# x^T of the first norm by block load and VectorE's block transpose, the norm folded into weights and exponential, and new PSUM places

## What is computed

```python
q, k, v = layernorm(x) @ Wq, ctx @ Wk, ctx @ Wv          # 8 heads of 64
x = x + (softmax(q k^T / 8) v) @ Wo + bo
h = layernorm(x)
rw = gating(h)                                           # softmax over active experts, at least 2
q, k, v = [sum_e rw_e * (h @ W_e) for W in (q_proj, k_proj, v_proj)]
a = softmax(causal(q k^T / 8)) v
x = x + sum_e (rw_e * a) @ o_proj_e
```

## Time and profile before

| | |
|---|---|
| runs, median of 3 | 2540.22 us |
| the profiled execution | 2538.06 us |
| its span, first to last instruction | 2536.3 us |
| mean granted TensorE clock | 0.987 |
| TensorE matmul busy | 2467.8 us, 97% |
| VectorE busy | 2124.7 us, 84% |
| ScalarE busy | 1558.2 us, 61% |
| GpSimd busy | 1102.7 us, 43% |
| TensorE's share of the chain that ended last | 81% |
| DMA queue of SP (q1), packets and share of the 16 engines | 230443, 45.6% |

### The profile page before, as it was taken

How to read it: one execution, slowest core, us unless ns; L and a number is a source line. 1 busy time by engine, 2 the same in 40 slices (tenths; PEclk the granted TensorE clock), 3 DMA queues, 4 the chain that set the end, 5 groups by cost and what they waited for, 6 DMA issues and landing times.

```text
span 2536.3 us, 54347 instructions
## 1 busy us (share of the span) xinstructions
PE 2467.8 (97%) x17180; PEld 2418.3 (95%) x17180; DVE 2124.7 (84%) x6190; ACT 1558.2 (61%) x5062; POOL 1102.7 (43%) x1741
## 2 busy tenths in 40 slices
PE   6799999999999999999999999999999999999997
PEld 5799999999999999999999999999999999999997
DVE  6788888888888888888888888888888888888885
ACT  6666666666666666666666666666666666666642
POOL 2244444444444444444444444444444444444442
PEclk7899999999999999999999999999999999999998
DMA  6765556465565556465565556465565556465531
GB/s 178 230 190 175 170 169 197 150 202 179 163 196 171 168 174 199 146 207 175 166 197 172 168 174 198 146 206 175 167 196 173 170 171 198 149 201 175 165 113 47
DMA packets 298312, 441.50 MB, mean 174 GB/s; under 512 B 31620, under 2 KB 209732, under 8 KB 289963
## 3 DMA queue, kind: packets, MB, share of 16 engines
q1 hardware_dynamic: 230443, 370.91, 45.6%
q10 hardware_dynamic: 67584, 67.12, 10.6%
HBM read 254.86 MB, written 181.83 MB: 172 GB/s over the span
## 4 chain that ended last, share of the span: by engine, by line
PE 81%; DVE 7%; POOL 5%; issue 3%; ACT 3%; DMA 0%; POOLq 0%; SPq 0%; ACTq 0%; DVEq 0%
PE bank_b L589 12%; PE bank_b L590 12%; PE bank_b L591 12%; PE bank_c L589 5%; PE bank_c L590 5%; PE bank_c L591 5%; PE bank_a L590 4%; PE bank_a L589 4%; PE bank_a L591 4%; PE bank_a L734 3%; PE bank_a L710 2%; PE bank_a L698 2%; DVE both L1424 2%; PE bank_a L699 2%; PE bank_a L673 1%
## 5 line engine op out<-in xcount | busy, mean ns | idle before, releaser
L1538 DVE SCALAR_TENSOR_TENSOR acc<-bank_b,rw,acc 128x192 f32<-128x192 f32 x1792 | 656.3, 407 | 106.0 <-PE bank_b L591 103.6
L589 PE MATMUL bank_b<-wqkv_hi,x2T_lo 128*128 128x384 f32 (+1 forms) x2048 | 715.4, 349 | 3.1 <-ACT acc L1142 1.9
L590 PE MATMUL bank_b<-wqkv_lo,x2T_hi 128*128 128x384 f32 (+1 forms) x2048 | 693.5, 339 | 0.0
L591 PE MATMUL bank_b<-wqkv_hi,x2T_hi 128*128 128x384 f32 (+1 forms) x2048 | 692.0, 338 | 0.0
L1112 ACT ACTIVATE probs<-bank_a,s_max 128x77 f32<-128x77 f32 x1024 | 317.3, 330 | 216.1 <-DVE s_max L1462 216.1
L1914 POOL TENSOR_TENSOR mixs_lo<-mix,mixs_hi 128x512 fp32r<-128x512 f32 x254 | 378.5, 1520 | 164.6 <-ACT mixs_hi L1212 164.6
L589 PEld LDWEIGHTS bank_b<-wqkv_hi,x2T_lo 128*128 128x128 f32 x2048 | 387.8, 189 | 4.1 <-ACT acc L1142 2.4
L590 PEld LDWEIGHTS bank_b<-wqkv_lo,x2T_hi 128*128 128x128 f32 x2048 | 387.8, 189 | 0.0
L591 PEld LDWEIGHTS bank_b<-wqkv_hi,x2T_hi 128*128 128x128 f32 x2048 | 385.8, 188 | 0.0
L1212 ACT ACTIVATE mixs_hi<-mix 128x512 fp32r<-128x512 f32 x256 | 160.0, 633 | 208.4 <-DVE mix L1579 208.4
L589 PE MATMUL bank_c<-wo_hi,mixs_lo 128*128 128x256 f32 x1000 | 281.9, 282 | 3.7 <-POOL mixs_lo L1914 3.7
(11 more groups left out here) (260 smaller groups left out, 6350.3 us busy)
## 6 DMA issues: line engine op xcount, KB each, us to landing
gq<-g_dram SPq DMA_DIRECT2D x63, 1232.0 KB, 5.5
rw_all<-rw_dram ACTq DMA_DIRECT2D x128, 512.0 KB, 7.1
uo<-u_dram SPq DMA_DIRECT2D x63, 1024.0 KB
g_dram<-draft SPq DMA_DIRECT2D x103, 462.0 KB
u_dram<-draft SPq DMA_DIRECT2D x127, 308.0 KB
g_dram<-mixs_lo SPq DMA_DIRECT2D x63, 462.0 KB
xt<-in_x_dram SPq DMA_DIRECT2D x64, 256.0 KB, 4.6
out_dram<-mix SPq DMA_DIRECT2D x62, 256.0 KB, 4.2
```

The costliest lines, as they stand in the source:

```text
L589: nc.tensor.matmul(dst, lhs[1], rhs[0], start=start, stop=False)
L590: nc.tensor.matmul(dst, lhs[0], rhs[1], start=False, stop=False)
L591: return nc.tensor.matmul(dst, lhs[0], rhs[0], start=False, stop=stop)
L1538: V.scalar_tensor_tensor(acc[:, t, k, :], src, rw[:, e, t:t + 1], acc[:, t, k, :], ALU.mult, ALU.add).then_inc(b_evac, 1)
```

## The change

Four things change together.

1. x^T is no longer transposed by TensorE. SP loads x a second time (`load_blocks`, four DMAs a batch of 32 partitions in pieces of 64 channels, 256 bytes), so that the 32x32 blocks lie where they belong, and one VectorE block transpose (`a_blocks`, L1411 of the changed kernel, 128x512) turns each block. The target and two of the three sources are parts of `probs`.
2. The first norm is folded. x^T holds raw x. The mean is taken out of Wq once in the opening (`query_weights`: VectorE sums each head's columns, scales, and ScalarE adds the negative mean). The scale 1/sqrt(var) and the 1/8 of the attention become the scale operand of the exponential, and VectorE multiplies the negative maxima by it (four operations of 128x4 a batch). `ln1_b`, its shift and `minus` of the first norm go.
3. The low part of x^T is made by GpSimd, after `a_xb`, the high part by ScalarE after slot L1 instead of after M1.
4. The PSUM places: XT keeps a place in `A_ORDER` but no bank use, and stands after M3. So M2 is in bank a0 (was a1), M3 in a1 (was a2); Y stays in a0, L1 in a1, L2 in a2. VectorE's calls for M2 and M3 are moved.

The diff, cut to its core:

```diff
-    A_ORDER = (..., "PT2", "E3", "M1", "XT", "M2", "M3", "Y", "L1", "L2")
+    A_ORDER = (..., "PT2", "E3", "M1", "M2", "M3", "XT", "Y", "L1", "L2")
...
+        x_cols, x_later = [probs[:, :, :].rearrange("p t c -> p (t c)")[:, s * CC * T:(s + 1) * CC * T] for s in range(2)]
+        def x_blocks(n):
+            return x_first if n == 1 else x_later
...
+            def load_blocks(n):
+                if n > 1:
+                    sp.wait_ge(pt_fill, at(3, n - 1, 2))
+                for k in range(4):
+                    sp.dma_start(x_blocks(n)[k * 32:(k + 1) * 32, :].rearrange("p (k c) -> p k c", k=TB),
+                                 x[n, :, :].rearrange("(k s) c -> s k c", s=32)[:, :, k * C // 4:(k + 1) * C // 4]).then_inc(xt_in[n % 2], 16)
...
                 turn(i, "E2")
+                if on(i + 2):
+                    load_blocks(i + 2)
                 turn(i, "E3")
...
-            def a_xT(n):
-                pe.wait_ge(ln_done[0], at(NT, n, NT - 1))
-                for cc in range(CC):
-                    for t in range(NT):
-                        last = nc.tensor.transpose(bank_xt(n)[...], xn[:, t, cc * P:(cc + 1) * P], ident[:, :])
...
+                    act.wait_ge(wq_mean_ready, k + 1)
+                    for e in range(2):
+                        last = nc.scalar.activation(wq[:, 2 * k + e, :], (banks_b[1:3] + banks_c)[k][:, e * C:(e + 1) * C], ACT.Identity,
+                                                    bias=wq_mean[:, 2 * k + e:2 * k + e + 1])
...
                     last = nc.scalar.activation(probs[:, t, h * NC:(h + 1) * NC], bank_s(n, j)[:, k * NC:(k + 1) * NC], ACT.Exp,
-                                                bias=s_max[:, j, k:k + 1], accum_out=p_sum[:, half, 0, t, k:k + 1])
+                                                bias=s_max[:, j, k:k + 1], scale=pow_out[0][:, 0, t:t + 1], accum_out=p_sum[:, half, 0, t, k:k + 1])
...
+            def a_blocks(n):
+                dve.wait_ge(xt_in[n % 2], 64 * (n // 2 + 1))
+                if n:
+                    dve.wait_ge(pt_fill, at(3, n - 1, 2))
+                V.transpose(x_cols.rearrange("p (a k s) -> p a k s", a=CC, k=TB),
+                            x_blocks(n).rearrange("p (k r a) -> p a k r", k=TB, a=CC)).then_inc(xt_fill, 1)
...
                 do(before, c_s)
+                turn(i, "M2")
                 do(before, c_p)
                 do(now, b_wsum)
-                turn(i, "M2")
                 do(ahead, a_y)
-                turn(i, "M3")
+                do(nxt, a_blocks)
                 do(before, c_pT)
                 do(now, b_qkv, 2)
                 do(now, b_rwT)
+                turn(i, "M3")
                 do(now, b_qkv, 3)
...
+            def a_xT(n):
+                pool.wait_ge(xt_hi, at(1, n, 0))
+                hi, lo = [t[:, :, :].rearrange("p a b -> p (a b)") for t in xT]
+                G.tensor_tensor(lo, x_cols, hi.bitcast(F32), ALU.subtract).then_inc(xt_evac, 1)
```

More of the change, by code:

```diff
@@ L39, in xattn_moe_kernel @@
     BIG = 3e38
-    A_ORDER = ("E0", "S0", "S1", "S2", "S3", "E1", "E2", "PT0", "PT1", "PT2", "E3", "M1", "XT", "M2", "M3", "Y", "L1", "L2")
+    A_ORDER = ("E0", "S0", "S1", "S2", "S3", "E1", "E2", "PT0", "PT1", "PT2", "E3", "M1", "M2", "M3", "XT", "Y", "L1", "L2")
     A_BANKS = 3
@@ L182, in xattn_moe_kernel @@
         rn = sb("rn", [P, 3, NT])
-        minus = [sb(f"minus{k}", [P, NT]) for k in (1, 2)]
-        shift = [sb(f"shift{k}", [P, NT]) for k in (1, 2)]
+        minus = sb("minus", [P, NT])
+        shift = sb("shift", [P, NT])
         ct = sb("ct", [TK, 2, 2 * P])
@@ L284, in xattn_moe_kernel @@
         xt_fill, xt_hi, xt_evac = sem("xt_fill"), sem("xt_hi"), sem("xt_evac")
+        xt_in, s_top = [sem(f"xt_in{k}") for k in range(2)], sem("s_top")
         s_fill = sem("s_fill")
@@ L302, in xattn_moe_kernel @@
         ln_pow = [sem(f"ln_pow{k}") for k in (1, 2)]
-        ln_done = [sem(f"ln_done{k}") for k in (1, 2)]
+        ln2_done, ln2_shift = sem("ln2_done"), sem("ln2_shift")
         rn_step = sem("rn_step")
@@ L319, in xattn_moe_kernel @@
         acc_opened = sem("acc_opened")
-        ln_shift = [sem(f"ln_shift{k}") for k in (1, 2)]
         passed = sem("passed")
@@ L606, in freed @@
                             return pe.wait_ge(y_evac, at(1, at_step + 1, 0))
-                    elif held == "XT":
-                        if on(at_step + 2) and at_step >= 0:
-                            return pe.wait_ge(xt_evac, at(1, at_step + 2, 0))
                     elif held[0] == "S":
@@ L614, in freed @@
                         return taken(*job(at_step, held))
-                return first_taken(*[held for held in OPENING if first_bank(*held) is bank_a(slot)][-1])
+                return first_taken(*[held for held in OPENING if held[0] != "xT" and first_bank(*held) is bank_a(slot)][-1])
             def first_taken(kind, f):
                 if kind == "xT":
-                    pe.wait_ge(xt_evac, at(1, f, 0))
-                elif kind == "s":
+                    return
+                if kind == "s":
                     pe.wait_ge(p_exp, at(2 * NT, f // (2 * NT), f % (2 * NT)))
@@ L870, in _ @@
                     j_u(0, f)
-                elif kind == "xT":
-                    a_xT(f)
                 elif kind == "s":
@@ L876, in _ @@
                         sim_norms()
-                else:
+                elif kind == "pT":
                     a_pT(0, f)
@@ L1164, in ln2_b @@
                     act.wait_ge(mix_lo, at(4, n - 2, 1))
-                ln_b(1, n, x2_tiles[n % 3], x2n)
+                act.wait_ge(ln2_shift, at(1, n, 0))
+                for t in range(NT):
+                    nc.scalar.activation(x2n[:, t, :], x2_tiles[n % 3][:, t, :], ACT.Identity, bias=shift[:, t:t + 1],
+                                         scale=pow_out[1][:, 0, t:t + 1]).then_inc(ln2_done, 1)
             def c_part(n, fill, dst, src):
@@ L1358, in query_weights @@
                 for k in range(HB):
+                    dve.wait_ge(wq_fill, k + 1)
+                    mean = wq_mean[:, 2 * k:2 * k + 2]
+                    V.tensor_reduce(mean, (banks_b[1:3] + banks_c)[k][:, :].rearrange("p (e c) -> p e c", e=2), AX.X, ALU.add,
+                                    negate=True).then_inc(wq_sum, 1)
+                    dve.wait_ge(wq_sum, k + 1)
+                    V.tensor_scalar(mean, mean, 1.0 / C, None, ALU.mult).then_inc(wq_mean_ready, 1)
+                for k in range(HB):
                     dve.wait_ge(wq_hi, k + 1)
@@ L1361, in query_weights @@
                         lo = wq[rows, 2 * k + e, :]
[L1362 to L1363 removed]
+                        last = V.scalar_tensor_tensor(lo, (banks_b[1:3] + banks_c)[k][rows, e * C:(e + 1) * C],
+                                                      wq_mean[rows, 2 * k + e:2 * k + e + 1], lo.bitcast(F32), ALU.add, ALU.subtract)
                 last.then_inc(wt_ready, 2)
```

85 lines of the change are left out of this document (36 added, 49 removed).

## The result

The changed kernel took 2768.78 us (median of 4 runs, 2765.06 to 2774.41) against 2539.77 us before (4 runs): a ratio of 1.0904, 95% interval 1.089 to 1.0918. Forecast were 2727 us, with a range of 2665 to 2825: slower, as forecast, and 42 us above the likeliest value.

The account below looks back on a forecast made before the run. TensorE, busy 97% of the span, was taken as the bound. Steps 133.7 us, opening 3 and clock 50 on the profiled 2538.1 us gave 2724.8, as a median 2727 us; range 2665 to 2825.

Parts of the forecast that it names:

- a_y's wait: Every step, a_y waits for M2's evacuation from their shared bank: 2.29 us after c_s against 0.46, 1.93 with restart.
- Rival (c): Banks are free when a_y and L1 ask, so no new waits: faster, 2496 us; chance 0.09.
- L1's wait: Every third step, L1 waits for M3's late evacuation from their shared bank: 3.33 us, +3.13 us with restart.
- net -0.55 us: Each step, TensorE loses the transposes of x, 0.73 us, but waits about 0.18 us at c_qk for GpSimd.
- The sum of the waits: Over steps 1 to 61: 41 at +1.06 us and 20 at +4.51 us, 133.7 us.
- What stays covered: Low part, load and four scalings (at most 0.25 us each, 1.69 us cover before PT0): nothing charged.
- rival (d): GpSimd's new subtraction delays VectorE's mix products by up to 1.3 us, and c_y with them: 2806 us; chance 0.06.
- The clock: Granted clock falls after L1's idle time, 2.5 us for each of 20: +50 us; nothing charged at a_y.
- Rival (a): Same waits at a_y and L1, but the clock never falls: 2677 us; chance 0.17.
- rival (b): The clock falls at a_y's wait too, 1.7 us for all 61: 2831 us; chance 0.20.
- The opening: VectorE sums and scales four halves of Wq^T before the first g job: +3 us, bounds 0 and 5.
- The block transpose: VectorE's new 128x512 operation, taken as 0.65 us; its bounds change the whole by -10 and +13 us.

Follow-up runs that it names:

- E2: Not a run: a slot in A_ORDER; PT2 takes the bank of E2's job, so it has no change or time of its own.
- the three suspects left out: Changed kernel with XT at its old place, x^T's low part only 32 columns wide, no scalings of the maxima, constant scale in the exponentials: 2538.39 us.

## Why the prediction was right, and where it was off

**a_y's wait** was right in cause, place and size: 2.29 us from c_s to a_y forecast, 2.23 measured; idle 1.67 us forecast, 1.6 measured; released by `both`. The places with VectorE's new order of calls, without any other part, produced it, and with XT at its old place it was gone. Rival (c), that the banks would be free, fell with the same rows.

**L1's wait** likewise: about 3.0 us idle forecast, 2.85 measured, released by `cT_lo`, in every third step.

**The transposes.** The step "net -0.55 us" took c_qk's wait for GpSimd into account at 0.18 us; the changed kernel shows 0.10 to 0.14 there. But the saving came out smaller: from b_xT to c_s three steps are 1.15 us shorter, 0.38 a step. The restart of 0.1 us behind that wait, which the prediction charged at a_y and L1, was not charged here. In the old places the same transposes cover a bank wait instead, which the prediction had no reason to price.

**The sum of the waits was too small.** Forecast were 6.63 us for three steps; at full clock the changed kernel takes 123.57 where it took about 114.1, 9.4 more. Over 61 steps that is 192 us, against the 134 of the sum. The failed step is "What stays covered": of the 2.8 us missing in three steps, 2.4 lie between PT0 and b_xT, and 0.5 are the transposes' smaller saving. It checked the scalings only against the path from GpSimd's probabilities to PT0, at 0.25 us each, and found 1.69 us of cover. There it was right: PT0 starts without a wait. What came late was another queue: ScalarE's copies for the jobs in E1 and E2, which stand behind the exponentials, and with them VectorE's evacuations that free the banks of PT1 and PT2. Three things delay it, and with XT at its old place each gave time back when it alone was left out (all four scalings 50 us, the column 21, the low part 31). The last scaling takes 0.87 us and not 0.19, whereas the first three take 0.23. That is its length, 0.85 us in the mean, beside GpSimd's product for the probabilities, in all 63 cases of the trace; the other 193 scalings take 0.23 to 0.26. In the rows below it ends as that product ends (552.87 + 1.22 = 554.09 and 553.24 + 0.87 = 554.11 us). How much of the 50 us is this wait and how much the scalings themselves wasn't separated. The exponentials take 0.093 us more each from start to start, which the prediction did not price at all: its text on the change has the new scale operand, and its sum nothing for it. And VectorE's products for the mix end late by the collision. Timelines of VectorE and GpSimd in the changed kernel:

```profile
552.70 0.43 DVE L1464 TENSOR_REDUCE s_max<-bank_a 128x4 f32<-128x308 f32 x1
553.24 0.87 DVE L1468 TENSOR_SCALAR s_max<-s_max,pow_out 128x4 f32<-128x4 f32 x1
```

```profile
552.87 1.22 POOL L1914 TENSOR_TENSOR probs<-probs,p_sum 128x616 f32<-128x616 f32 x1 [2.15 <-DVE p_sum L1474]
```

**The collision** was rival (d), with a chance of 0.06. It happens, in about two of three steps. Its size was overdrawn (up to 1.3 us; 0.72 measured), and so was its consequence, c_y late by all of it: c_y doesn't wait, and the low part was worth 31 us where nothing else hid it.

**The clock** was over-priced: 50 us forecast, 2.5 us for each of 20 waits, from two gaps near the start (3.4 and 1.7 us lost), where work was thin around them. Measured are about 1.4 us for three steps, 28 us. Rival (a), no fall at all, and rival (b), a fall at a_y's wait too, are both refuted: the stretch at 910 us shows the lower level after 2.85 us of idling, and the kernel with M3 evacuated early shows none in the middle of the span with a 1.6 us wait in every step. Rival (b) was nearer than that sounds: 1.67 us were forecast for a_y's wait, 1.60 lowered nothing, and 1.72 and 1.89 us did in two steps.

**The opening** was +3 us with 5 as the upper bound; the first a_y starts at 79.8 us instead of 71.2, 8.6 more. With the three suspects left out it is 75.9, so some 4.6 us come with the weights and the load; the rest goes with those three.

**The block transpose** was 0.65 us in the sum and takes 0.70; that is nothing.

Together: waits +58 us, clock -22, opening +6, and about 4 in the rest (1.3 of them behind the last a_y) make the 46 us between the 2724.8 of the sum and the 2770.5 of the profiled execution. Two errors of opposite sign partly cancelled. Direction and most of the size came for the reason given, the two bank waits. That the range also had room for the 58 us is luck: its upper part was kept for a falling clock, and the term that filled it was put at nothing.

## What to carry to other kernels

Before a slot of a ring is moved, write down for each slot who held its bank last and when that holder's evacuation stands in the evacuating engine's order; a removed slot shifts all the others, and two near neighbours in one bank can cost their whole evacuation in every step. A factor folded into an operand isn't free: it appears on the engine that now applies it, here as 16 longer exponentials and 4 small operations a step. When small work is added to an engine that is 80% busy, check every queue behind it, here the copies and subtractions that free banks, and not only the one consumer of the value.
